# A transformer layer pair with routed experts: one program for layer one and its 72 routed tiles, and a new order of its steps

## The reference, cut to what matters

```python
# L1_cond: eo is the typed expert's result, s0 and s1 those of two shared experts
s0 = _dense(x, swi[0], swo[0]); s1 = _dense(x, swi[1], swo[1])      # relu(x @ wi_) @ wo_, 128 -> 512 -> 128
gate_in = jnp.concatenate([eo[:, 0], s0[:, 0], s1[:, 0]], axis=-1)
w = jax.nn.softmax(jax.nn.relu(gate_in @ g1) @ g2, axis=-1)          # three weights for each sequence
c = eo * w[:, 0] + s0 * w[:, 1] + s1 * w[:, 2]
# L1_ffn: attention with 16 heads of 8 over 32 tokens, then the two best of eight routed experts
h = _layernorm(c, ln1_g, ln1_b); q, k, v = split(h @ w_qkv + b_qkv)
x2 = c + softmax(q @ k.T / sqrt(8)) @ v @ w_o + b_o
h = _layernorm(x2, ln2_g, ln2_b); logits = h @ gate_w + gate_b
topv, topi = jax.lax.top_k(logits, 2); gw = softmax(topv)
moe = sum over the two of gw * (relu(h @ W1[e] + b1[e]) @ W2[e] + b2[e])
out = x + x2 + moe
```

## Time and profile before

| what | value |
|---|---|
| three runs | 684.72, 680.09, 682.74 us; median 682.74 |
| the profiled execution | 685.2 us, its span 683.4 us |
| TensorE busy | 563.6 us (82%), mean granted clock 0.928 |
| VectorE (DVE), ScalarE (ACT), GpSimd (POOL) busy | 403.1, 383.1, 333.3 us |
| traffic with memory | 30.30 MB read, 22.62 MB written, 77 GB/s |

### The profile page before, as it was taken

The page is one execution under the profiler, slowest core; times in us unless marked ns, Lnnn a source line. Parts: engine busy times, 40 slices in busy tenths (PEclk is TensorE's granted clock), DMA queues, the critical chain, the costliest instruction groups (busy, mean ns, idle before and its releaser), DMA issues. The chain is left out here.

```text
span 683.4 us, 18201 instructions
## 1 busy us (share of the span) xinstructions
PE 563.6 (82%) x5428; PEld 433.8 (63%) x5429; DVE 403.1 (59%) x1407; ACT 383.1 (56%) x792; POOL 333.3 (49%) x372
## 2 busy tenths in 40 slices
PE   1578999866699992999999999898988929999950
PEld 1233555434699991666666666566778829999950
DVE  6235888994433321045767777768777554655636
ACT  0225767775466631457466566565756707888830
POOL 1236477774100002343456767665558734777750
PEclk9998999995799996899999999998999977999995
DMA  8920011111622210010533221213312222222229
GB/s 274 316 40 1 15 36 39 36 62 58 186 64 69 62 28 4 16 44 21 158 77 139 64 63 34 56 48 73 72 45 71 69 67 61 73 72 72 72 60 341
DMA packets 72071, 54.03 MB, mean 79 GB/s; under 512 B 25816, under 2 KB 63520, under 8 KB 71600
## 3 DMA queue, kind: packets, MB, share of 16 engines
q1 hardware_dynamic: 60400, 34.36, 18.3%
q0 software_dynamic: 6432, 13.25, 6.0%
q10 hardware_dynamic: 5152, 5.34, 2.4%
HBM read 30.30 MB, written 22.62 MB: 77 GB/s over the span
## 5 line engine op out<-in xcount | busy, mean ns | idle before, releaser
L1309 POOL DMA_INDIRECT rows_dram<-u_row,u_slots x64 | 62.6, 978 | 38.9 <-DVE u_slots L2192 22.3
L1446 PE MATMUL u_py<-u_hh,cwo 128*128 128x512 f32 x128 | 64.1, 595 | 0.0
L2474 POOL DMA_INDIRECT y_dram<-x_y,x_to x48 | 48.2, 1003 | 27.3 <-DVE x_y L2580 26.5
L1797 ACT ACTIVATE u_hh<-u_pz 128x512 f32<-128x512 f32 x64 | 36.7, 596 | 36.4 <-PE u_pz L1438 36.1
L2510 PE MATMUL x_py<-w,x_h 128*128 x384 | 51.6, 278 | 0.1
L2569 DVE TENSOR_SCALAR x_h<-x_pc,p_bT 128x128 f32<-128x128 f32 x96 | 29.5, 347 | 36.2 <-PE x_pc L2500 35.9
L2510 PEld LDWEIGHTS x_py<-w,x_h 128*128 128x128 f32 x384 | 47.6, 195 | 0.3 <-issue 0.3
L1263 POOL DMA_INDIRECT u_eo<-eo_dram,type_slot x1 | 1.0, 1027 | 84.7 <-issue 84.7
L2539 ACT ACTIVATE x_held_w<-w 128x512 f32 x48 | 30.2, 630 | 19.4 <-PEq L1217 12.8
L788 POOL DMA_INDIRECT xs_dram<-x,type_slot x32 | 31.6, 987 | 17.8 <-DVE x L702 10.0
L953 PE MATMUL e_py<-cwt,e_h 128*128 x288 | 38.5, 277 | 0.9 <-issue 0.7
(11 more groups left out here) (370 smaller groups left out, 1640.0 us busy)
## 6 DMA issues: line engine op xcount, KB each, us to landing
w<-in_mw SPq DMA_DIRECT2D x2, 2048.0 KB, 8.4
x_xs<-rows_dram SPq DMA_DIRECT2D x48, 65.0 KB
cwt<-in_cw SPq DMA_DIRECT2D x1, 2560.0 KB, 10.4
xs_dram<-zero SPq DMA_DIRECT2D x1, 2304.0 KB, 16.6
e_xs<-xs_dram SPq DMA_DIRECT2D x36, 64.0 KB, 1.9
eo_dram<-e_y SPq DMA_DIRECT2D x36, 64.0 KB, 1.6
x_dram<-x SPq DMA_DIRECT2D x8, 256.0 KB, 2.0
x1t<-x_dram SPq DMA_DIRECT2D x8, 256.0 KB, 4.7
```

The source lines that it names most:

```text
L1309: pool.indirect_dma_start(rows_dram, bass.IndirectOffsetOnAxis(ap=slots[:, q, k, u:u + 1], axis=0), row[:, q, k, u, :], None).then_inc(sen ...
L1446: nc.tensor.matmul(py[:], cwo[:, m * KF + k], hh[:, e % HR], start=(m == 0 and k == 0), stop=(m == NSH - 1 and k == KF - 1)).then_inc(s_ma ...
L1797: act.activation(hh[:, e % HR], pz[e % 2][:], ACT.Relu).then_inc(hh_made, 1)
L2474: pool.indirect_dma_start(y_dram, bass.IndirectOffsetOnAxis(ap=to[t % R][:], axis=0), y[:, t % R, :], None).then_inc(sent[t % R], 16)
```

## The change

The function `experts` is gone; layer_one does all 72 tiles (ET), in that program's banks: tiles from AT on use one set of banks for even t and another for odd t (`second_banks`). XR is 12, and the result buffers lie in the shared experts' hidden buffer. For t below AT ACT takes all four quarters of the hidden numbers, in banks that alternate; from AT on ACT and DVE take two each. The bias product of every tile is on DVE. The end clears are all on SP, behind the load of tile 19 and ahead of that of tile 20. `deal` is cut in six steps on DVE, after tile 17's result, and the scatters of tiles from 23 on stand behind the wait for all `sent`.

The shared experts' inputs are no longer weighted: one `turn_x`, one `high` (ACT) and one `low` (DVE) for each block. `second` has the hidden numbers as the stationary operand, four times 128 columns, and sums for each shared expert apart, so the sum comes out by tokens; `sums` and `turn_back` are gone. DVE weights the first sum and adds the typed expert's part (`middle`), and `mix` does the second. POOL weighs the typed expert's result (`weigh`, 1 for a block where 2 were). The chain for `wtok` is cut in pieces in iterations -1 and 0. Each step `scores` is in four parts with steps `first` and `second` between them. `deal_early` is cut in nine steps. The first eight tile loads stand ahead of the store and load of block 6's values on SP. All orders are written anew; block 4's second four sends come after the loop.

```diff
-XR = 3
+XR = 12
...
-        experts(nc, sb, pb, sem, ident, expert_of_tile, row_of_tile, row_low, row_high, rows_dram, y_dram, biases, bT)
...
+        vy = hh[:].rearrange("p r (u d) -> p (r u) d", d=D)[:, 0:XR]
...
+        def second_banks(t):
+            return t >= AT and t % 2 == 1
+
+        def va(t):
+            return pgh[0] if second_banks(t) else pz[0]
+
+        def vc(t):
+            return pgh[1] if second_banks(t) else pz[1]
+
+        def vo(t):
+            return pf if second_banks(t) else py
+
+        def pv(t):
+            return pt_ if second_banks(t) else pe_
...
+                    if t == AT:
+                        sp.wait_ge(dealt, 2)
+                        sp.wait_ge(tail_sent, 16 * E)
...
+                def clear_end(e):
+                    if e == 0:
+                        sp.wait_ge(ended, 1)
+                    o = sp.value_load(runi[0:1, e:e + 1], min_val=0, max_val=ROWS - P)
+                    sp.dma_start(rows_dram[bass.ds(o, P), :], none[:]).then_inc(tail_sent, 16)
+
+                for i in range(NB - 2):
                     store_v(i)
                     load_v(i)
...
                 for t in range(VU):
                     load_row(t)
-                store_v(NB - 1)
-                load_v(NB - 1)
-                for t in range(VU, AT):
+                for i in range(NB - 2, NB):
+                    store_v(i)
+                    load_v(i)
+                for t in range(VU, AT - 4):
+                    load_row(t)
+                for e in range(E):
+                    clear_end(e)
+                for t in range(AT - 4, ET):
...
+                    pool.tensor_tensor(ew[:, i % 2], eo[:, i % 2], wtok[:, tiles_of(i), 0:1].to_broadcast([P, SB, D]), ALU.mult)\
+                        .then_inc(ew_made, 1)
...
+                    if ok(i + 2):
+                        gather(i + 2)
+                    if ok(i - 2):
+                        carried(i - 2)
                     if ok(i - 3):
                         added(i - 3)
-                    if ok(i):
-                        gather(i)
+                    if ok(i - 4):
+                        scatter(i - 4, 1)
...
+                send(NB - 4, 1, 0)
+                send(NB - 4, 1, 1)
+                send(NB - 4, 1, 2)
+                added(NB - 3)
+                carried(NB - 2)
                 carried(NB - 1)
...
                 for q in range(RB):
                     pool.wait_ge(sent[q], 16 * 2 * SB * len(range(q, NB, RB)))
+                for t in range(AT - 1, ET):
+                    scatter_row(t)
...
                 def second(i, m, k):
                     e = NH * i + KF * m + k
                     pe.wait_ge(hh_made, e + 1)
-                    if m == 0 and k == 0:
+                    if k == 0:
                         claim("y")
-                        free["y"] = (yT_made, i + 1)
-                    nc.tensor.matmul(py[:], cwo[:, m * KF + k], hh[:, e % HR], start=(m == 0 and k == 0),
-                                     stop=(m == NSH - 1 and k == KF - 1)).then_inc(s_made, 1)
-
-                def turn_back(i):
-                    pe.wait_ge(yT_made, i + 1)
-                    claim("turns")
-                    for u in range(SB):
-                        last = nc.tensor.transpose(pt_[:, u * D:(u + 1) * D], yT[:, u * P:(u + 1) * P], ident[:])
-                    last.then_inc(y_turned, 1)
-                    free["turns"] = (c_made, i + 1)
+                        free["y"] = (c_made, i + 1) if m else (mid_made, i + 1)
+                    for u in range(SB):
+                        last = nc.tensor.matmul(py[:, u * D:(u + 1) * D], hh[:, e % HR, u * P:(u + 1) * P], cwo[:, m * KF + k],
+                                                start=(k == 0 and u == 0), stop=(k == KF - 1 and u == SB - 1))
+                    last.then_inc(s_made, 1)
...
+                def scores(i, h, u):
+                    if u == 0:
+                        pe.wait_ge(qT_made, i + 1)
+                        pe.wait_ge(km_made, i + 1)
+                        claim("g0")
+                        claim("g1")
+                    for b in range(BT):
+                        t = slice((u * BT + b) * S, (u * BT + b + 1) * S)
+                        for g in (2 * h, 2 * h + 1):
+                            r = slice(g * GW, (g + 1) * GW)
+                            last = nc.tensor.matmul(pgh[g % 2][b * S:(b + 1) * S, u * P:(u + 1) * P], qT[r, t], km[r, :, t],
+                                                    start=True, stop=True)
+                    if u == SB - 1:
+                        last.then_inc(scored, 1)
...
+                    if t < AT:
+                        parts = ((pz[t % 2], va_summed, range(KF)),)
+                        after(pe, va_made, t - 1)
+                    else:
+                        parts = ((va(t), va_summed, range(KH)), (vc(t), vc_summed, range(KH, KF)))
...
                     if ok(i):
                         second(i, 0, 0)
                     if ok(i - 2):
-                        turn_p(i - 2, 0)
-                    if ok(i):
-                        first(i, 0, 3)
-                        turn_x(i, 1)
-                    if ok(i - 2):
-                        turn_p(i - 2, 1)
+                        scores(i - 2, 1, 0)
                     if ok(i):
                         second(i, 0, 1)
+                    if ok(i - 2):
+                        scores(i - 2, 1, 1)
+                    if ok(i):
                         second(i, 0, 2)
+                    share(i)
...
+                second_row(17)
                 turn_row(19)
-                second_row(16)
                 first_row(18)
                 turn_row(20)
-                second_row(17)
                 first_row(19)
                 turn_row(21)
...
+                for t in range(AT, ET + 1):
+                    if t < ET:
+                        first_row(t)
+                    if t + 2 < ET:
+                        turn_row(t + 2)
+                    second_row(t - 1)
...
+                    z, ks = (pz[t % 2], range(KF)) if t < AT else (va(t), range(KH))
+                    for k in ks:
+                        last = act.activation(vh[:, t % 2, k * P:(k + 1) * P], z[:, k * P:(k + 1) * P], ACT.Relu,
                                               bias=bT[:, bass.ds(named[t] * KF + k, 1)])
                     last.then_inc(va_made, 1)
...
+                def middle(i):
+                    if i == 0:
+                        dve.wait_ge(wtok_made, 1)
+                    dve.wait_ge(s_made, NH * i + KF)
+                    dve.wait_ge(ew_made, i + 1)
+                    after(dve, c_made, i)
+                    for u in range(SB):
+                        last = nc.vector.scalar_tensor_tensor(mid[:, u], py[:, u * D:(u + 1) * D], wtok[:, i * SB + u, 1:2],
+                                                              ew[:, i % 2, u], ALU.mult, ALU.add)
+                    last.then_inc(mid_made, 1)
...
                     after(dve, cb_made, i - 1)
                     for u in range(SB):
-                        last = nc.vector.scalar_tensor_tensor(cres[:, i % 2, u], eo[:, i % 2, u], wtok[:, i * SB + u, 0:1],
-                                                              pt_[:, u * D:(u + 1) * D], ALU.mult, ALU.add)
+                        last = nc.vector.scalar_tensor_tensor(cres[:, i % 2, u], py[:, u * D:(u + 1) * D], wtok[:, i * SB + u, 2:3],
+                                                              mid[:, u], ALU.mult, ALU.add)
...
+                weigh_row(19)
+                deal(0)
+                deal(1)
+                deal(2)
+                deal(3)
+                deal(4)
+                result_row(18)
+                deal(5)
...
+                for t in range(AT, ET + 1):
+                    if t < ET:
+                        hidden_row(t)
+                        weigh_row(t)
+                    result_row(t - 1)
```

More of the change, by code:

```diff
@@ L1656, in _ @@
                     if ok(i + 1):
-                        turn_x(i + 1, 0)
+                        turn_x(i + 1)
+                    gate(i, 0)
+                    if ok(i - 1):
+                        scores(i - 1, 0, 1)
+                    if ok(i):
+                        first(i, 1, 3)
+                    if ok(i - 1):
+                        scores(i - 1, 0, 2)
+                    if ok(i):
+                        second(i, 1, 2)
+                    if ok(i - 1):
+                        scores(i - 1, 0, 3)
@@ L1692, in _ @@
+                query(NB - 1)
+                turn_p(NB - 2, 2)
                 first_row(2)
+                value_rows(NB - 1)
+                counts(NB - 3)
+                turn_p(NB - 2, 3)
+                attend(NB - 2)
                 turn_row(3)
+                second_row(2)
+                first_row(3)
+                turn_o(NB - 2)
+                scores(NB - 1, 0, 0)
                 turn_row(4)
-                scores(NB - 1, 0)
```

(50 more changed lines are left out.)

957 lines of the change are left out of this document (392 added, 565 removed).

## The result

The changed kernel takes **702.63 us** (median of 4 runs, 702.06 to 705.13); the kernel before took 683.31 beside it (4 runs). The ratio is 1.030, 95% interval 1.027 to 1.033: 3% slower, where 672 was forecast. The profiled execution took 705.13 and spans 703.1.

A forecast was written before the change was run, and what follows sets the result against it. TensorE was taken to bound the loop and the last 48 tiles, no engine the stretch between. Result 24 earlier by 11.7 and +1 for the last tiles gave -10.7 on 685.2: 674.5, median 672 us; range 655 to 688.

The forecast's parts named there:

- Start: Block 0's first `first`, no longer behind the `wtok` chain, starts at about 265.7 instead of 273.30: -7.6 us.
- Scores in four parts: Each scores step split in four costs TensorE +1.0 us; thirteen steps in the loop: +13.3, bounds 0 and +16.
- Rival B: The split of the scores is free, so 13.3 us come back: 658 us; chance 0.24.
- Shared products: Two turns go per block, eight `second` cost +0.03 each: -0.62 a block, -4.9 us over eight blocks.
- `deal_early`: In nine pieces behind other DVE work in the loop: -2.6 us, bounds 0 and -2.6.
- The loop: The loop, up to its end, finishes 1.8 us earlier, at about 464.
- The bound I gave: Sign for the loop: the prediction is wrong if an iteration takes over 28.5 us; 27 to 28 was expected.
- After the loop: Following POOL's queue with its 11.6 us idle kept: `root2` of block 7 at 520, slots at 530, T0 about 536.
- T0: When `deal` can begin after the loop: 553.5 before, forecast about 536; past 545 the prediction is wrong.
- rival C: After the loop, `root2` of block 7 on POOL is late: T0 555, result 24 at 578.5, median 691; chance 0.11.
- The end clears: Eight clears on SP take 9 us; TensorE stands from about 538 to 547 at `turn_row(20)`; result 24 at 559.5.
- Last 48 tiles: TensorE's work unchanged, bias product on DVE adds 0.34 a tile: +1 us in all, bounds 0 and +5.

The follow-up runs named there:

- number 4: The changed kernel with three edits: scores steps whole, loads of tiles 20 to 23 ahead of the end clears, `value_rows` behind `divided`; 675.18 us, ratio to before 0.986.
- numbers 1 and 4: Number 1: the changed kernel with each scores step in one piece again, 696.94 us, ratio to before 1.019; number 4 has its own line.
- number 3: The changed kernel with DVE's `value_rows` moved from the iteration's end to behind `divided`; 695.90 us, ratio to before 1.020.
- Number 2: The changed kernel with loads of tiles 20 to 23 ahead of the eight clears on SP's queue; 691.01 us, ratio to before 1.009.

## Why the prediction was wrong

- **Start:** right. The first product came at 264.7, where 265.7 was forecast; forecast -7.6, measured -9.7 at `mix` 0.
- **Scores in four parts:** the price is right: 1.47 for part and `second` against 1.49, 1.2 for a step from `mix` 0 to `mix` 1, and 11.2 us of TensorE's busy time in the loop between number 4 (171.1) and the changed kernel (182.3), where 13.3 were forecast. (13 steps at 1.07 are 13.9, not 13.3.) But taking it back gives 5.6 to 8.4 us, not 13, as TensorE then meets waits on DVE that the parts had covered. Rival B (free) was wrong.
- **Shared products:** right, 0.03 for a `second`. With whole scores at full clock (numbers 1 and 4) a full iteration ahead of `deal_early` has TensorE busy 25.7 to 26.0 us, where before had 26.1; -0.6 was forecast.
- **`deal_early`:** right but for 0.4: the iteration with it takes 29.1, the one before 28.7.
- **Stops and waits in the loop:** missing from the sum. From `mix` 0 to `mix` 7 the forecast's terms make TensorE busy 179.4 us and idle 2.7; it was busy 182.3 and idle 8.0, of which 4.1 are stops in short products. What the other 2.9 of busy time are is not worked out. A further stop of 2.2 stands in `attend` 6. No row of the trace of before shows one in the loop. In the forecast I had counted every queue of POOL for its own time, never for what its DMAs do to others.
- **The loop** was to end 1.8 earlier than before and ended 4.2 later: 6.0 of the 31.4 us between forecast (result 24 at 559.5) and measurement (590.9). The bound I gave, 28.5 us an iteration, was passed.
- **After the loop: this step failed.** T0 was to be 536, from POOL's queue. It was 555.1, rival C's time; that the two meet is luck, as C had block 6's slots as late as before (509.6) and they came at 519.4. From `mix` 7 to T0 82.9 us were measured where 69.8 were forecast: 13.1. POOL issued just the 29 indirect DMAs that I had counted ahead of `root2` of block 7, and from that root to the slots were 10.1 us (forecast 10.0). The term that was wrong is POOL's idle time ahead of that root, which I had left at the 11.6 of before: it was about 23 from `mix` 7 on, of which 6.3 and 5.4 are waits for `u_x` of blocks 6 and 7. The attention chain was late, not POOL. Of the 13.1, 6.1 are TensorE at `turn_row(0)` for `u_vtok` (number 3 took 5.3 us out of this stretch), and 2.2 the stop; 4.8 remain, in an order that has sixteen early results before the slots of block 7 (550.4), where before had eleven (526.2). I followed the one engine that was bound before and not the chain through the others.
- **The end clears: this step failed too.** The place and the wait were right. T0 to result 24 took 35.8 against 23.5, 12.3 of the miss. The hole itself ended 12.7 behind T0 where 11 were forecast, 1.7. The other 10.6 lie behind it: from there to result 24 were 12.5 in the sum, for four tiles on ACT and one more product and result, and 23.1 measured, because results 18 and 19 were still to come (`second_row(18)` stood behind the turns of tiles 20 to 23; they came at 577.9 and 581.4), with TensorE at a mean granted clock of 0.84. Number 2 took 13.9 back with a swap of two loops.
- **Last 48 tiles:** right; the bias product on DVE costs nothing (1.88 a tile; forecast +1).

6.0 + 13.1 + 12.3 make the 31.4. The three edits take 27.5 back.

## What to carry to other kernels

Cost a reordered kernel by following the chain through every engine's written order, not the one queue that was bound before: here one DVE pass written last (6.1 us) and eight clears ahead of four loads that did not need them (13.9) outweighed all that the change won. Ask of each step that is put behind another whether its input is made by then: `second_row(t)` right behind `first_row(t)` doubled the time of a tile (3.6 against 1.8). Ask of each indirect DMA on POOL what runs beside it on TensorE, above all runs of short products. And try a kernel that is within 2% of its rival on more than one chip: number 4 stood 1.4% under the kernel before on one and 2.7 to 2.9% over it on three others.

## What the hardware showed that I had not expected

- Beside POOL's indirect DMAs (scatters and gathers) TensorE's short products stop, with no wait in the profile: `attend` 1.30 us alone, 1.6 to 3.5 beside two or three scatters in the loop on the first kind of chip, 11.2 to 11.4 for seven scatters on the second (blocks 2 and 3 in every one of its profiles of number 4), 7.0 to 7.2 for four. What is short in it (instruction supply, a port) is open: the products' own duration stays, the spacing grows.
- ACT, DVE and SP show the like on the second kind: 8.2 to 8.3 us "remote" on ACT behind T0 in every profile of number 4, beginning while POOL issues the last sends (the last of them 5.1 behind T0), and 6.2 on DVE in one iteration of before. Beside the same sends SP's eight clears take 11.6 instead of 8.8. No experiment addressed them.
- Chips differ: the kernel before took 683 and 685 in two sets of runs and 739 to 744 on four other chips, with one iteration of its loop at 37.4 us instead of 26.2. Its two profiles differ from `mix` 0 to T0 alone, 322.0 us against 261.9; what is ahead (290.5 and 291.6) and behind (128.6 and 129.9) is the same. That is the stretch with the scatters of rows; that the stops make up all of the 60 us is not shown. The clock does not explain an `attend` at 11.2: granted clock was 0.56 there, which would at most double 1.3.
- A second kind of stop, 2.1 to 2.7 us, sits in `attend` 0 with no scatter near and was gone in both profiles of the stream shifted by 128 instructions. A 16 KB fetch begins beside it in all thirteen profiles that have it; that this is the cause is likely, and not shown, as the same fetch beside `attend` 5 stops nothing.
